# Graph layer on one core: three landing slots instead of four from stripe 9 on, and a quarter of 132 late cells multiplied in three fp32r passes

## What is computed

```python
def _L0_gnn_ref(x, adj, W):
    A_hat = adj + jnp.eye(adj.shape[0], dtype=adj.dtype)
    d_inv_sqrt = jnp.sum(A_hat, axis=1) ** (-0.5)
    A_norm = d_inv_sqrt[:, None] * A_hat * d_inv_sqrt[None, :]
    support = x @ W.T
    out = A_norm @ support
    return jax.nn.relu(out)
h = jnp.maximum(_layernorm(x, axis=-1), 0.0)
x = x + _L0_gnn_ref(h, adj, L0_gnn_W)
```

## Time and profile before

| | us |
|---|---|
| median of 3 runs | 1192.61 |
| lowest, highest run | 1184.71, 1192.80 |
| the profiled execution | 1185.19 |
| its span, first to last instruction | 1183.4 |
| TensorE busy | 949.1 (80%) |
| VectorE busy | 838.8 (71%) |
| ScalarE busy | 553.6 (47%) |
| GpSimd busy | 128.8 (11%) |

### The profile page before, as it was taken

One profiled execution on the slowest core, in us unless ns is written; L12 is line 12 of the kernel. 1 busy time (PEld: TensorE's weight loads), 2 busy tenths in 40 slices (PEclk: granted clock), 3 DMA queues, 4 the chain that ended last, 5 costly groups with the idle time before them and its releaser, 6 DMA issues.

```text
span 1183.4 us, 9349 instructions
## 1 busy us (share of the span) xinstructions
PE 949.1 (80%) x2363; PEld 434.0 (37%) x2363; DVE 838.8 (71%) x1081; ACT 553.6 (47%) x1655; POOL 128.8 (11%) x102
## 2 busy tenths in 40 slices
PE   1713053483768879899998999999999999899997
PEld 1511021131323334344443444444444444344443
DVE  7952043373656867788887888888888888787785
ACT  0766675667655755462735626226246272100011
POOL 4021020110210101010101010000010000010011
PEclk9966576786979899999999999999999999999999
DMA  9999999999899999999999999999999799999993
GB/s 336 370 400 344 364 389 335 320 319 359 300 365 366 339 350 347 306 367 343 328 332 336 337 316 368 342 270 314 309 264 287 205 330 287 281 274 322 337 337 94
DMA packets 260486, 381.33 MB, mean 322 GB/s; under 512 B 10449, under 2 KB 237905, under 8 KB 260433
## 3 DMA queue, kind: packets, MB, share of 16 engines
q1 hardware_dynamic: 130288, 190.40, 51.3%
q10 hardware_dynamic: 130144, 190.34, 50.6%
HBM read 376.50 MB, written 4.19 MB: 322 GB/s over the span
## 4 chain that ended last, share of the span: by engine, by line
PE 43%; ACT 3%; DMA 3%; ACTq 1%; DVE 1%; SPq 1%; issue 0%; POOLq 0%; POOL 0%; DVEq 0%
PE bank L508 42%; DMA slot<-in_adj_dram 3%; ACT junk L547 2%; ACTq L289 1%; ACTq L297 1%; DVE adjT L701 0%; PE pre L484 0%; ACT slot L537 0%; ACT kept_cell L565 0%; SPq L342 0%; SPq L335 0%; DVE kept_cell L787 0%; POOLq L190 0%; POOL kept_cell L439 0%; SPq L289 0%
## 5 line engine op out<-in xcount | busy, mean ns | idle before, releaser
L508 PE MATMUL bank<-adjT,support 128*128 128x512 f32 x2048 | 908.2, 605 | 177.8 <-DVE adjT L701 177.7
L508 PEld LDWEIGHTS bank<-adjT,support 128*128 128x128 f32 x2048 | 394.4, 194 | 669.6 <-issue 666.4
L701 DVE STREAM_TRANSPOSE adjT<-slot 128x1024 f32<-128x1024 f32 x430 | 526.5, 1237 | 108.6 <-PE bank L508 97.2
L547 ACT ACTIVATE junk<-slot 128x384 bf16<-128x384 f32 (+2 forms) x732 | 348.1, 477 | 256.6 <-issue 144.9
L537 ACT ACTIVATE slot<-slot 128x6144 f32<-128x6144 f32 (+11 forms) x56 | 166.4, 2971 | 158.8 <-issue 74.7
L685 DVE TENSOR_REDUCE part<-slot 128x4 f32<-128x1536 f32 (+2 forms) x61 | 95.2, 1562 | 133.1 <-DMA slot<-in_adj_dram 133.1
L547 ACT ACTIVATION_READ_ACCUMULATOR junk<-slot 128x1 f32 x732 | 136.5, 186 | 0.0
L701 DVE STREAM_TRANSPOSE adjT<-kept_cell 128x1024 f32<-128x1024 f32 x70 | 85.0, 1231 | 27.6 <-PE bank L508 27.6
L428 POOL COPY kept_cell<-slot 128x2048 f32<-128x2048 f32 x35 | 65.1, 1892 | 352.5 <-DVE adjT L701 352.5
L565 ACT ACTIVATE kept_cell<-kept_cell,dinv 128x128 f32<-128x128 f32 x64 | 20.2, 389 | 176.1 <-DVE adjT L701 86.7
L416 POOL TENSOR_TENSOR dinv<-total,power 128x4 f32<-128x4 f32 x16 | 16.1, 1007 | 477.5 <-DVE total L755 477.5
(11 more groups left out here) (53 smaller groups left out, 166.3 us busy)
## 6 DMA issues: line engine op xcount, KB each, us to landing
slot<-in_adj_dram ACTq DMA_DIRECT2D x134, 768.0 KB, 13.3
slot<-in_adj_dram SPq DMA_DIRECT2D x134, 768.0 KB, 14.5
slot<-in_adj_dram ACTq DMA_DIRECT2D x66, 512.0 KB, 11.7
slot<-in_adj_dram SPq DMA_DIRECT2D x66, 512.0 KB, 12.6
slot<-in_adj_dram ACTq DMA_DIRECT2D x8, 1536.0 KB, 20.6
slot<-in_adj_dram SPq DMA_DIRECT2D x8, 1536.0 KB, 21.2
slot<-in_adj_dram SPq DMA_DIRECT2D x4, 1408.0 KB, 14.3
slot<-in_adj_dram ACTq DMA_DIRECT2D x4, 1408.0 KB, 15.0
```

Of the source, the lines that this page charges most:

```text
L508: ins = nc.tensor.matmul(bank[bank_of(g)][:], support[:, v * R + t, :], adjT[at % TURNS][:, r, :], start=(n == first_of[g] and t == 0), st ...
L547: nc.scalar.activation(junk[at % JUNKS][:, :n], cells[:, c, :], ACT.Copy, accum_out=part[u % 2][:, k, c:c + 1]).then_inc(junk_done, 1)
L701: nc.vector.transpose(adjT[at % TURNS][:].rearrange("p t (c i) -> p t c i", i=Q), half.rearrange("p c (t r) -> p t c r", r=Q)).then_inc(t_ ...
```

## The change

1. From piece 63 on (the first left piece of stripe 9) there are three slots: `slot_of` is (m - 63) mod 3, and ScalarE issues piece m + 2 where it issued m + 3. The near piece of stripe 9 and everything before keep four slots.
2. The memory of slot 3, and of the three `adjT` buffers beside it, is taken over by `low` (three halves), `s_parts` (for each of the 16 blocks two 128 x 128 tiles, high and low part of the last tile of `support`) and `high` (two buffers of 128 x 512). GpSimd may write them once slot 3 is free (`slot_free`, at cell 75).
3. For 132 cells from cell 78 on (the list `parted`; all later cells but those at which GpSimd has other work) GpSimd splits the last 128 columns of the transposed cell: `high` is the fp32r rounding of them (a `CAST`), `low` the rest (a `TENSOR_TENSOR` subtract). Both stand between the second transpose of the cell and the last quarter of its product.
4. For these quarters TensorE runs three fp32r matmuls of 128 x 512 instead of one fp32 matmul: high x high, low (of support) x high, high x low (of the cell). The product low x low is left out. The other three quarters of the cell stay fp32.
5. GpSimd's program is no longer by stripe but follows `order`; copies, root and the adds of `x` have places in it. In the tail the stores are put where these adds now are (`added_at`). Of the 132 cells 4 are in stripe 9, then 13, 15, 21, 17, 14 and 12 in stripes 10 to 15, and 36 in the tail.

```diff
@@ the ring
-    slot_of = [m % SLOTS for m in range(len(landing))]
+    THREE = next(m for m in range(far[SPLIT_FROM][0], len(landing)) if m % SLOTS == SLOTS - 1)
+    slot_of = [m % SLOTS if m < THREE else (m - THREE) % (SLOTS - 1) for m in range(len(landing))]
+    LAST_OF_FOUR = max(m for m in range(len(landing)) if slot_of[m] == SLOTS - 1)
@@ which cells
+    copy_at = [0] + [column_at[u - 1] + 2 for u in range(1, NB)]
+    other_work = {n for u in range(NB) for n in (copy_at[u], copy_at[u] + 1, totals_at[u], scale_at[u], scale_at[u] + 1)}
+    PARTS_AT = min(n for n in range(len(order)) if order[n][2] is not None and order[n][2] >= THREE + 2)
...
+    other_work |= {added_at(n) for n in range(NB)}
+    parted = [n for n in range(PARTS_AT + 3, len(order)) if n not in other_work]
@@ ScalarE
-                load_piece(act, (2, 3), m + AHEAD)
+                if m + SLOTS - 1 < THREE:
+                    load_piece(act, (2, 3), m + SLOTS - 1)
+                elif m + SLOTS - 2 >= THREE:
+                    load_piece(act, (2, 3), m + SLOTS - 2)
@@ GpSimd
+            def part_tile(n):
+
+                k, at = parted.index(n), HALVES * n + HALVES - 1
+                tile = adjT[at % TURNS][:, R // HALVES - 1, :]
+                pool.wait_ge(t_done, transposed(n))
+                if k >= 2:
+                    pool.wait_ge(used, transposed(parted[k - 2]))
+                nc.gpsimd.tensor_copy(high[:, k % 2, :], tile).then_inc(high_ok, 1)
+                pool.wait_ge(high_ok, k + 1)
+                nc.gpsimd.tensor_tensor(low[:, at % TURNS, R // HALVES - 1, :], tile, high[:, k % 2, :].bitcast(F32),
+                                        ALU.subtract).then_inc(low_ok, 1)
...
+            for n in range(len(order)):
+                for u in range(NB):
+                    if n == copy_at[u]:
+                        copies(u)
+                    if n == totals_at[u]:
+                        root(u)
...
+                if n in parted:
+                    part_tile(n)
+                if added < NB and n >= added_at(added):
+                    add_x(added)
+                    added += 1
@@ TensorE
+                        if n in parted and t == R - 1:
+                            i = parted.index(n)
+                            pe.wait_ge(s_parted, v + 1)
+                            pe.wait_ge(low_ok, i + 1)
+                            nc.tensor.matmul(bank[bank_of(g)][:], s_parts[:, v, 0, :], high[:, i % 2, :], start=False, stop=False)
+                            nc.tensor.matmul(bank[bank_of(g)][:], s_parts[:, v, 1, :], high[:, i % 2, :], start=False, stop=False)
+                            ins = nc.tensor.matmul(bank[bank_of(g)][:], s_parts[:, v, 0, :], low[:, at % TURNS, r, :],
+                                                   start=False, stop=last)
```

71 lines of the change are left out of this document (50 added, 21 removed).

## The result

The changed kernel takes 1228.11 us (median of four executions; 1224.91 to 1230.27) against 1192.61 (also four): the ratio is 1.031, with a 95% interval of 1.026 to 1.036, 35.5 us slower by the medians. The forecast was 1198.5, its range 1177 to 1220, so the result lies outside it. The profiled execution took 1228.71 us, 43.5 more than the one of before.

The account below looks back on a forecast made before the run. It took TensorE to bound the kernel from 540 us on, loads close behind: 28.3 us saved, 5 + 19.8 + 5.4 + 4 = 34.2 given back, 5.9 net loss, so 1198.5 us on the median, range 1177 to 1220.

Parts of the forecast that it names:

- the ring: Load slots from stripe 9 on, three for four: 19.8 us at stripes, 4 in the tail, 5.4 for lower clock.
- the saving: Last quarters of 132 cells on TensorE: 0.215 us saved per cell, 28.3 us in all.
- the splits: GpSimd's work for parted cells: mostly hidden, late behind some sums in stripes 11 to 15, 5 us lost.
- The bound: From 540 us on TensorE bounds the kernel, with loads close behind at the starts of stripes 9 to 11.
- The passes: TensorE in parted cells: one fp32r pass 0.215 us, three 0.644 against 0.859 for fp32; 28.3 us saved.
- the fourth rival: TensorE in parted cells: an fp32r pass takes 0.43 us; about 65 us slower, 1258; chance 0.06.
- The split: GpSimd between second transpose and last quarter: 2.06 us, hidden except 0.33 us late at about 15 places, 5 us.
- Three slots: Loads from stripe 9 on lose one piece of lead: harmless in steady parts, 19.8 us lost around stripe starts.
- the upper end: Stripes 9 to 15: waits drag the next loads with them, costing 35 us instead of 19.8.
- The clock: TensorE at new gaps in stripes 10, 12 and 15: half clock costs 1.8 us each, 5.4 us.
- The tail: After stripe 15: four loads of three cells 1 us late each, 4 us; moved adds and stores cost nothing.
- The second rival: Stripes 9 on and tail: waiting for slots becomes the bound; 27 us slower, 1220; chance 0.22.

Follow-up runs that it names:

- e5: Kernel before with its four slots; 132 cells end in three fp32r passes over a constant tile, nothing split: 1176.03 us, ratio 0.990.
- e4: Changed kernel with three slots, its fp32r passes over a constant tile and no split of the adjacency: 1222.62 us, ratio 1.024.
- e11: Changed kernel with passes over constant tiles, while GpSimd still does 132 splits of a constant tile that nobody reads: 1224.79 us, ratio 1.028.
- e1: Changed kernel with no parted cells: three slots, all matmuls fp32, additions in their new places: 1230.92 us, ratio 1.035.
- e6: Kernel before, four slots, all fp32; from piece 63 on ScalarE issues each load one piece later: 1202.64 us, no ratio given.
- e10: Changed kernel with x not loaded again in the tail, GpSimd adding y to y: 1232.52 us, ratio 1.029.
- e9: Three slots, all fp32, no splits, plus a fourth slot for the first piece of each of stripes 10 to 15: 1213.2 us, ratio 1.019.

## Why the forecast was wrong

The forecast gave back 34.2 us for 28.3 saved. By the steps of the traces three things were mis-sized: the ring by 16 us, the saving by 15, the splits by 8.

*The bound*, TensorE from 540 us on with the loads close behind, was right for the kernel before. The sentence drawn from it failed: "an instruction saved on TensorE can count in full". With three slots the loads bound the kernel in TensorE's place so often that of the 21 us of e5 only 13 arrive in e4.

*The passes*: 0.215 us forecast for one, 0.225 to 0.23 measured, which makes 22 us instead of 28.3. With the 8 us that do not arrive the term is 13. That fp32r is not at the fp32 rate of the fourth rival was right: a pass of 0.43 us at full clock is excluded.

*The split*: 0.6 forecast for the cast, 0.61 measured; the subtraction 1.27 and 1.27. Late by 0.33 after a sum: six rows of 0.34 us stand in TensorE's waits before the tail, all in pieces whose load was late, and the step of 3.82 us above. These waits are 2.0 us (14.4 less the 12.4 of the tail), but they leave out delays in which TensorE already loads weights. Counted from start to start, 24 cells before the tail have the first pass at the split's end and are together 5.5 us late, where 5 us at 15 places were forecast. So this price was about right; what the sum left out is GpSimd's work beside VectorE's, up to 7 us in e11, and the tail.

*Three slots*: this is the step that failed most. 19.8 us for the stripes, 4 for the tail and 5.4 for the clock make 29.2; e1 measured 39 by the medians and 45 by the steps. The mechanism stands: "Each load keeps its time and loses one piece of lead" is what the table under e6 shows. What failed is what was made of it.

- "In the steady part of a stripe that is harmless: two pieces of three cells are 19 us, a load takes 13.5." The 13.5 is the median of one queue's loads. Until the last part of a piece lands 15 us pass in the kernel before, and the lead is 16.9 us and not 19. The median slack between landing and use over stripes 13 to 15 fell from 10.8 us to 1.5, so each small delay became a wait.
- The late loads were not those listed. The third left piece of stripe 15 was right: 7.2 us late forecast, 6.98 measured. For the near piece of stripe 12 VectorE waits 2.67 us (4.3 forecast), for that of stripe 10 5.97 (4.3). The first left piece of stripe 9 was to cost 4.1 and is in time: it goes out at 489.4 us (491.2 before), into the slot of the stripe's first far piece; the 498.63 of the forecast is the issue of the second left piece. In stripe 13 the load behind the near slot is in time, as forecast, but VectorE waits 2.39 us for the second left piece and 3.01 for the fourth (843.37). The first left piece of stripe 15 was not looked at: 4.07 us at 945.99.
- A late load makes the next ones late. In stripe 13 the load behind the near slot goes out at 819.93, when GpSimd has copied; ScalarE's sums of the first left piece stand behind it and end at 826.2, and the load that needs this piece's slot goes out at 826.49, though VectorE had left the slot at 821.9. That is the load that is 3.01 us late. The forecast had this as the upper end only ("if the waits drag the next loads with them", 35).

Together VectorE's waits for loads from 480 us on went from 13.1 us to 49.0, and to 63.2 in e1; TensorE's idle time in the same stretch grew by 32 us in e1 (13.5 to 45.5) where 24 were forecast.

*The clock*: three gaps of 1.8 us were forecast. TensorE now waits 15 times for VectorE, up to 7.5 us, and the granted clock is 0.97 over all three stretches. Some 20 us stand for the 5.4; in e1, without passes or splits, 13 (45.4 less the 32 of idle time), an estimate.

*The tail*: "The new places of the adds and stores cost nothing" failed. They stand ahead of loads that can wait, but on GpSimd they now stand ahead of splits that cannot: up to 9 us (e10). The loads themselves cost about 5 (e1), 4 forecast.

The second rival had the direction and the place (the ring), 1220 with chance 0.22. Its price for the ring, 35 + 5.4 + 10 = 50.4 us, is above what e1 measured; it came out 8 us short because it too took the saving at 28.3 and the splits at 5.

## What to carry over

Price a ring by when each slot comes free: work out the time from that moment to the use of the next piece in the slot, and set it against the time until the last part of a load lands, not against the median of one queue. The place of the load in the issuing program can matter little (e6). A piece that waits for a second reader takes a slot out of the round; in stripes 13 to 15 a slot for it alone took all of VectorE's waits for loads away (e9), while stripes 10 to 12 kept more than half of their loss and the tail all of it. A saving on the busiest engine counts in full only as long as nothing else comes to bound it; here the same change took the slack away. And an engine that had slack gets a queue order when work with a deadline is put on it: whatever already stood there and may wait must go behind.

## What the runs showed of the hardware

An fp32r pass over 512 columns with its own weights takes 0.225 to 0.23 us at a granted clock of 1.00 (730 to 745 us in the changed kernel), and 0.42 us at 0.50 (1092 to 1094 us); each of the two records of an fp32 matmul takes 0.43 at 1.00. GpSimd's cast of 128 x 512 from fp32 to fp32r takes 0.61 us. VectorE's `TENSOR_SCALAR` of 128 x 128 takes 0.277 us in e4 and 0.455 in e11 and the changed kernel, where GpSimd splits beside it, while its transposes stay at 1.23 (1.235 before).
